# Normalising the softmax rows on GpSimd, and transposing them one group later

## The chip, the cores and the metric

The kernel runs on one core of a Trainium2 chip. The metric is the device time of one execution in microseconds (us). Most executions of a kernel agree within 0.3%. The engines are named as in the profile: PE is TensorE's matmuls and PEld its weight loads, DVE is VectorE, ACT is ScalarE, POOL is GpSimd, SP is the queue that only issues DMAs.

## The reference, cut to what matters

The input is x, 4 x 64 x 32 x 32. Two layers are computed: a Mamba-like convolution and scan block, then causal attention, and last a layer of 33 steps, each with a table of 19 sets of weights. A step picks its set by an argmax over the state, and masks say whether it does its attention, its feed-forward part, both or neither:

```python
def step(h, p):
    op = jnp.argmax(h[0, 0, :NOPS])
    q, k, v = h @ p['wq'][op], h @ p['wk'][op], h @ p['wv'][op]
    attn = jax.nn.softmax(jnp.einsum('bqd,bkd->bqk', q, k) * scale, axis=-1)
    y = jnp.einsum('bqk,bkd->bqd', attn, v) @ p['wo'][op]
    h = jnp.where(p['am'][op], y, h)
    z = jax.nn.relu(h @ p['w1'][op] + p['b1'][op]) @ p['w2'][op] + p['b2'][op]
    h = jnp.where(p['fm'][op], z, h)
    return (h, None)
```

With the inputs used here one step's attention runs, between two feed-forward parts. There are four sequences of 1024 tokens with 64 channels, all in float32. The attention has no causal mask.

## The kernel before, in words

Engines run their own programs and wait for each other through semaphores; the order of the work on each engine is written out by hand. Channels lie on partitions, two sequences at a time (rows r = 0 on partitions 0 to 63, r = 1 on 64 to 127), so that the four sequences are 2 x 2048 columns. One class, `Attention`, serves the causal attention of the layer before (`causal=True`, one pass, driven by code of its own) and that of the last layer (`ea`, `causal=False`), whose drivers are `pe_all`, `dve_all` and `act_all`. It goes over GRP = 16 groups g of 128 queries. For each group and each r:

- `pe_scores` (L242): four matmuls of 512 columns write the scores of 128 queries against 1024 keys into PSUM, `s[0]` and `s[1]` (`pb` in the trace). There is one pair of these tiles, so scores(g) wait until both exps of group g − 1 have read them.
- `dve_max_halves` (L343, L347, L349): row maxima, negated. For r = 0 two halves and their minimum, for r = 1 one pass over 1024.
- `act_exp` (L402): the exp of the scores into `p[g % 2][r]` in SBUF (`bb`, `dbu`), with the row sums in `sm`. Its read of the accumulator is an instruction of its own.
- `dve_inverse` (L367): `rc` = 1 / `sm`, for both r.
- `pe_turn` (L279): eight transposes of 128x128 of one `p` into the PSUM tile `pt` (`py`), of which there is one, 128 x 1024. Each half of four transposes is signalled on its own. Turn r = 1 may write a half once `dve_turned` has copied that half of r = 0 out, and the next r = 0 once the halves of r = 1 are out.
- `dve_turned` (L355) copies both halves of r = 0 into `pts` (`da`, `cc`), `act_turned` (L410) the first half of r = 1 and `dve_turned_rest` (L361) the second.
- `pe_values` (L292, L302): first two matmuls spread the inverse sums over partitions (L292: `rc` broadcast to 64 columns as weights, the identity as data) into columns 128 to 255 of the bank `ob` or `rb` (`px`), then 16 matmuls multiply the values `vv` with `pts` into columns 0 to 127.
- `act_inverse` (L416) copies the spread inverse to `rs`, and `output` (L107) multiplies the values' product by it. `finish` calls it three groups later.

In the steady state TensorE's order is scores(g), turn(g − 1, 1), values(g − 2), turn(g, 0). `hand_over` (L1764) copies four finished groups of output at a time. GpSimd has an empty `pool_attend`; what it does in this layer are sums of 512 columns in the feed-forward part (L1970). Behind the attention comes the feed-forward part, whose first TensorE work is L1044.

Of the kernel before, what the change touches and what calls it, by code (L numbers as in the profile page):

```python
# [45 lines left out]
class Attention:  # L46
# [4 lines left out]
    def __init__(self, nc, ctx, w, causal, bufs=None):  # L51
        tag = "l1_" if causal else "ex_"

        def sb(name, shape):
            return ctx.enter_context(nc.sbuf_tensor(tag + name, shape, FP32))

        def ps(name, shape):
            return ctx.enter_context(nc.psum_tensor(tag + name, shape, FP32))

        def sem(name):  # L60
            return ctx.enter_context(nc.semaphore(tag + name))

        self.nc, self.w, self.causal = nc, w, causal
        if bufs is None:
            bufs = {"qt": sb("qt", [128, T2C]), "kt": sb("kt", [128, T2C]), "vv": sb("vv", [128, self.GRP, 2, C]),
                    "p": [[sb(f"p_{a}{r}", [128, L]) for r in range(2)] for a in range(2)],
                    "pts": [[sb(f"pts_{a}{r}", [128, L]) for r in range(2)] for a in range(2)],
                    "rs": sb("rs", [128, 2, 128]), "nm": sb("nm", [128, 4]), "mh": sb("mh", [128, 2]), "sm": sb("sm", [128, 4]), "rc": sb("rc", [128, 4]),
                    "s": [ps(f"s_{r}", [128, L]) for r in range(2)], "pt": ps("pt", [128, L]),
                    "ob": ps("ob", [128, HALF]), "rb": ps("rb", [128, HALF])}  # L70
        self.qt, self.kt, self.vv, self.p, self.pts = (bufs[name] for name in ("qt", "kt", "vv", "p", "pts"))
        self.rs, self.nm, self.mh, self.sm, self.rc = (bufs[name] for name in ("rs", "nm", "mh", "sm", "rc"))
        self.s, self.pt, self.ob, self.rb = (bufs[name] for name in ("s", "pt", "ob", "rb"))
        self.q_full, self.q_out = sem("q_full"), sem("q_out")
        if causal:
            self.k_full, self.k_out = sem("k_full"), sem("k_out")
        else:
            self.fold_full, self.fold_act, self.fold_dve = sem("fold_full"), sem("fold_act"), sem("fold_dve")
        self.v_full, self.v_act, self.v_dve = sem("v_full"), sem("v_act"), sem("v_dve")
        self.s_full, self.nm_done, self.p_done = sem("s_full"), sem("nm_done"), sem("p_done")  # L80
        self.turned, self.pts_dve, self.pts_act = sem("turned"), sem("pts_dve"), sem("pts_act")
        self.rc_done, self.o_full, self.o_out = sem("rc_done"), sem("o_full"), sem("o_out")
        self.rb_out = sem("rb_out")


    def prime(self, eng, *counts):
# [6 lines left out]
            pe.sem_inc(sem, count)  # L93

    def prime_act(self, act):
        for sem, count in ((self.q_out, 2), (self.fold_act, 2), (self.v_act, 2), (self.p_done, 2 * self.GRP), (self.pts_act, self.GRP), (self.rb_out, self.GRP)):
            act.sem_inc(sem, count)

    def prime_dve(self, dve):
# [3 lines left out]

    def output(self, dve, k, g, to):

        dve.wait_ge(self.rb_out, self.GRP * k + g + 1)
        self.nc.vector.tensor_tensor(to, (self.ob, self.rb)[g % 2][:, 0:128], self.rs[:, g % 2, :], ALU.mult).then_inc(self.o_out, 1)  # L107

    def blocks(self, g):
        return g % 8 + 1 if self.causal else L // 128  # L110
# [144 lines left out]
    def pe_turn(self, pe, k, g, r):  # L255

        nc = self.nc
        pe.wait_ge(self.p_done, 2 * (self.GRP * k + g) + r + 1)
        if g == 0 and r == 0 and not self.causal:
            for c in (2, 3):  # L260
                self.query_ready(pe, k, c)
# [21 lines left out]
    def pe_values(self, pe, k, g, early=None):  # L283
        nc, p, bank = self.nc, g // 8, (self.ob, self.rb)[g % 2]
        if g == 0 and not self.causal:
            pe.wait_ge(self.v_dve, 2 * k + 2)
            pe.wait_ge(self.v_act, 2 * k + 2)
        pe.wait_ge(self.rc_done, self.GRP * k + g + 1)
        atleast(pe, self.o_out, self.GRP * k + g - 1)
        for r in range(2):  # L290
            i = 2 * (g % 2) + r
            nc.tensor.matmul(bank[C * r:C * r + C, 128:256], self.rc[:, i:i + 1].broadcast_to((128, C)),  # L292
                             self.w["cst"][:, IDN:IDN + 128], start=True, stop=True)
# [12 lines left out]
    def pe_all(self, pe, k, src, wa, turned_w, v_wait):  # L306
        for g in range(self.GRP):
# [9 lines left out]
                self.pe_project_v(pe, k, src, wa[2], (0, 1))  # L317
            else:
                self.pe_scores(pe, k, g)
                self.pe_turn(pe, k, g - 1, 1)  # L320
            if g >= 2:
                self.pe_values(pe, k, g - 2)
            self.pe_turn(pe, k, g, 0)
            if g == 0:
                self.pe_project_v(pe, k, src, wa[2], (2, 3))
        self.pe_turn(pe, k, self.GRP - 1, 1)
        self.pe_values(pe, k, self.GRP - 2)
        self.pe_values(pe, k, self.GRP - 1)


    def dve_max(self, dve, k, g, r):
# [30 lines left out]

    def dve_inverse(self, dve, k, g):
        dve.wait_ge(self.p_done, 2 * (self.GRP * k + g) + 2)
        atleast(dve, self.o_full, self.GRP * k + g - 1)
        i = 2 * (g % 2)
        self.nc.vector.reciprocal(self.rc[:, i:i + 2], self.sm[:, i:i + 2]).then_inc(self.rc_done, 1)  # L367

    def dve_all(self, dve, k, wa, turned_w, finish, hand_over):
        last = self.GRP - 1  # L370
        for g in range(self.GRP):
            if g == 0:
                self.dve_fold(dve, k, turned_w[1], turned_w[2], wa[2])
            if 3 <= g < last:
                finish(dve, k, g - 3)
            self.dve_max_halves(dve, k, g)
            if g == 0:
                self.dve_project(dve, k, 3)
                self.dve_project_v(dve, k, (0,))
            else:  # L380
                self.dve_turned_rest(dve, k, g - 1)
            self.dve_turned(dve, k, g)
            self.dve_inverse(dve, k, g)
            if g == 0:
                self.dve_project_v(dve, k, (2,))
            if g in (10, 12):
                hand_over(dve, k, g // 2 - 5)
            if g == last:
                hand_over(dve, k, 2)
                finish(dve, k, g - 3)  # L390
        self.dve_turned_rest(dve, k, last)
        for g in range(last - 2, last + 1):
            finish(dve, k, g)
# [24 lines left out]
    def act_all(self, act, k, wa, turned_w):  # L418
        for g in range(self.GRP):
            if g == 0:  # L420
                self.act_fold(act, k, turned_w[0], wa[0])
                self.act_project(act, k, 0)
                self.act_project(act, k, 2)
            else:
                self.act_turned(act, k, g - 1)
            for r in range(2):
                self.act_exp(act, k, g, r)
            if g == 0:
                self.act_project_v(act, k, (1, 3))
            if g >= 2:  # L430
                self.act_inverse(act, k, g - 2)
        self.act_turned(act, k, self.GRP - 1)
        self.act_inverse(act, k, self.GRP - 2)
        self.act_inverse(act, k, self.GRP - 1)


def build_all(nc, w, inp, scr, out):

    ctx = ExitStack()
    with ctx:  # L440
# [1529 lines left out]
            nc.gpsimd.tensor_tensor(fin[c], t2[:, col(c)], hn[:, col(c)], ALU.add).then_inc(fin_done if c < NCH - 1 else fin_last, 1)  # L1970

        def pool_attend(pool, k, kf, e, n):
            pass

        def pool_feed(pool, k, ka, e, n, b):
            for c in range(NCH - 1):
# [28 lines left out]

        @block.gpsimd
        def _(pool):
            nc.gpsimd.memset(w["eps"][:, :], EPS).then_inc(ones_set, 1)
            nc.gpsimd.memset(w["mone"][:, :], -1.0).then_inc(ones_set, 1)
            nc.gpsimd.memset(natl[:, NP_:NV + 1, :], 0.0).then_inc(nat_set, 1)  # L2010
# [243 lines left out]
```

## Time and profile before

| what | value |
|---|---|
| time, median of 3 runs | 708.53 us (707.62 to 711.39) |
| the profiled execution, its own time | 711.64 us |
| its span | 709.8 us |
| mean granted TensorE clock | 0.961 of full speed |
| PE busy | 618.5 us, 87% |
| DVE busy | 581.7 us, 82% |
| ACT busy | 415.2 us, 59% |
| POOL busy | 451.1 us, 64% |

The span is the stretch between the profiled execution's first and last instruction, the time has what lies around it as well. Busy shares are means over the whole span, most of which is the scan of the first layer; the last layer begins at about 555 us. The profile names tiles by the buffers that they share: `pb` are the scores, `bb` and `dbu` are `p`, `py` is `pt`, `da` and `cc` are `pts`, `px` holds the outputs, `gate_all` the small columns (maxima, sums, inverses, `rs`), `w_xs` the attention's output.

### The profile page before, as it was taken

Reading aid. Unit: us, or ns where it says so; the run is one execution under the profiler, and the core shown is the slowest. Engines: PE = TensorE matmul, PEld = TensorE weight load, DVE = VectorE, ACT = ScalarE, POOL = GpSimd, SP = SyncE. Lnnn points to the kernel's source line nnn. Section 1 sums busy time; section 2 is a strip of 40 time slices with the busy share of each in tenths; the row PEclk is TensorE's granted clock in tenths of the full one; section 3 lists DMA queues with packets and bytes.
Section 4 is the critical chain, followed back from the end, with each engine's and each line's share of the span. In section 5 each row is a group of like instructions: output and inputs, shape, how many; then the busy total and the mean of one; then the engine's idle time right before and its main releaser. Section 6 shows DMA issues by size and latency. Waiting matters only on the chain.

```text
span 709.8 us, 10911 instructions
## 1 busy us (share of the span) xinstructions
PE 618.5 (87%) x3732; PEld 267.0 (38%) x3732; DVE 581.7 (82%) x622; ACT 415.2 (59%) x643; POOL 451.1 (64%) x240
## 2 busy tenths in 40 slices
PE   8889879889877888988878887988979999999996
PEld 3323222222222212222222222345756446777771
DVE  5799999999999999999999999364365457788755
ACT  4878777668567566766774663353445525544441
POOL 7599999999999999999999999510000220000002
PEclk9989999999999999989999999999899999999999
DMA  3876679686666675666666763000000000000001
GB/s 104 220 267 211 230 227 291 226 259 226 232 232 253 211 250 211 236 217 210 234 233 222 234 241 115 1 1 0 3 5 8 1 20 1 1 2 1 2 2 65
DMA packets 32107, 101.20 MB, mean 143 GB/s; under 512 B 6821, under 2 KB 7342, under 8 KB 32046
## 3 DMA queue, kind: packets, MB, share of 16 engines
q1 hardware_dynamic: 30486, 99.42, 41.6%
q10 hardware_dynamic: 1240, 0.88, 0.4%
q8 instruction: 33, 0.54, 0.3%
q14 instruction: 28, 0.23, 0.1%
q0 software_dynamic: 320, 0.13, 0.1%
HBM read 94.64 MB, written 2.10 MB: 136 GB/s over the span
## 4 chain that ended last, share of the span: by engine, by line
PE 44%; DVE 23%; issue 19%; ACT 7%; POOL 5%; DMA 1%; DVEq 0%; ACTq 0%; POOLq 0%
DVE hh_all L1641 9%; DVE pb L1636 8%; PE py L279 7%; PE pb L242 6%; PE px L302 5%; PE py L816 5%; POOL hc L1956 4%; PE pb L1044 2%; PE py L1068 2%; PE px L845 2%; PE pb L804 2%; POOL dbu L1967 2%; PE px L292 1%; DVE dtu_all L1615 1%; PE px L763 1%
## 5 line engine op out<-in xcount | busy, mean ns | idle before, releaser
L1956 POOL TENSOR_TENSOR hc<-hh_all,cc 128x1024 f32<-128x1024 f32 x128 | 298.5, 2355 | 6.3 <-DVE hh_all L1641 4.6
L1641 DVE TENSOR_TENSOR_SCAN hh_all<-da,pb 128x1024 f32<-128x1024 f32 x80 | 182.9, 2286 | 3.4 <-ACT da L1324 0.4
L1970 POOL TENSOR_TENSOR yg<-w_xs 128x512 f32<-128x512 f32 x10 | 12.6, 1266 | 227.1 <-DVE w_xs L1783 132.7
L816 PE MATMUL py<-hc,w_cst 64*64 64x512 f32 x1024 | 148.2, 639 | 8.5 <-DVE yg L1652 8.5
L1967 POOL TENSOR_TENSOR dbu<-bb,dtu_all 128x1024 f32<-128x1024 f32 x48 | 113.2, 2358 | 5.0 <-DMA bb<-scr 5.0
L1641 DVE TENSOR_TENSOR_SCAN hh_all<-pb,dbu 128x1024 f32<-128x1024 f32 x48 | 108.9, 2269 | 2.0 <-DVE dtu_all L1615 1.7
L1636 DVE TENSOR_TENSOR pb<-pb,dtu_all 128x1024 f32<-128x1024 f32 x80 | 97.1, 1214 | 3.7 <-PE pb L804 1.2
L804 PE MATMUL pb<-bc,w_sel 128*128 128x512 bf16 x160 | 51.8, 408 | 53.1 <-DVE hh_all L1641 53.0
L1324 ACT ACTIVATE da<-dt_all,w_aneg 128x1024 f32<-128x1024 f32 x80 | 89.8, 1138 | 2.7 <-DVE dt_all L1622 1.8
L1324 ACT ACTIVATE pb<-dt_all,w_aneg 128x1024 f32<-128x1024 f32 x48 | 53.6, 1116 | 64.3 <-DVE hh_all L1641 63.8
L816 PEld LDWEIGHTS py<-hc,w_cst 64*64 64x64 f32 x1024 | 31.2, 136 | 80.9 <-issue 54.4
L804 PEld LDWEIGHTS pb<-bc,w_sel 128*128 128x128 bf16 x160 | 11.0, 99 | 113.4 <-DVE hh_all L1641 83.8
L335 DVE TENSOR_REDUCE gate_all<-pb 128x1 f32<-128x128 f32 (+7 forms) x32 | 22.8, 752 | 19.6 <-PE pb L252 19.5
L279 PE MATMUL py<-w_cst,dbu 128*128 128x128 f32 x208 | 30.3, 286 | 8.1 <-ACT dbu L402 4.8
L402 ACT ACTIVATE bb<-pb,gate_all 128x1024 f32<-128x1024 f32 (+4 forms) x32 | 28.6, 898 | 7.8 <-DVE gate_all L335 7.8
L402 ACT ACTIVATE dbu<-pb,gate_all 128x1024 f32<-128x1024 f32 (+3 forms) x32 | 30.3, 952 | 4.8 <-DVE gate_all L335 4.8
L242 PE MATMUL pb<-w_xs,u_all 64*128 64x512 f32 x128 | 31.8, 615 | 0.0
L410 ACT ACTIVATE da<-py 128x512 f32<-128x512 f32 (+2 forms) x20 | 9.8, 510 | 37.3 <-PE py L279 37.1
L410 ACT ACTIVATE cc<-py 128x512 f32<-128x512 f32 (+1 forms) x20 | 10.7, 553 | 34.6 <-PE py L279 34.6
L355 DVE COPY da<-py 128x512 f32<-128x512 f32 (+2 forms) x28 | 16.1, 610 | 17.6 <-PE py L279 17.6
L279 PE MATMUL py<-w_cst,bb 128*128 128x128 f32 x192 | 27.2, 279 | 3.8 <-ACT bb L402 3.8
L279 PEld LDWEIGHTS py<-w_cst,dbu 128*128 128x128 f32 x208 | 23.2, 144 | 19.1 <-issue 12.4
(326 smaller groups left out, 1020.0 us busy)
## 6 DMA issues: line engine op xcount, KB each, us to landing
cc<-scr SPq DMA_DIRECT2D x128, 512.0 KB, 4.3
bb<-scr SPq DMA_DIRECT2D x48, 512.0 KB, 5.0
w_xs<-w_xm SPq DMA_DIRECT2D x8, 256.0 KB, 6.5
w_xs<-hc SPq DMA_DIRECT2D x6, 256.0 KB, 3.8
scr<-bcf SPq DMA_DIRECT2D x8, 128.0 KB, 4.6
out<-yg SPq DMA_DIRECT2D x4, 256.0 KB, 2.6
w_xst<-in_x SPq DMA_DIRECT2D x1, 512.0 KB, 4.6
w_cst<-in_consts ACTq DMA_DIRECT2D x1, 404.0 KB, 5.0
```

Of the source, the lines that this page charges most:

```text
L242: part = nc.tensor.matmul(self.s[r][:, o + a:o + a + m], self.qt[rows, g * 128:(g + 1) * 128], self.kt[rows, p * L + a:p * L + a + m], sta ...
L279: last = nc.tensor.transpose(self.pt[:, o + j:o + j + 128], self.p[g % 2][r][:, j:j + 128], self.w["cst"][:, IDN:IDN + 128])
L302: last = nc.tensor.matmul(bank[C * r:C * r + C, 0:128], self.vv[:, p * 8 + j, r, :], self.pts[g % 2][r][:, j * 128:(j + 1) * 128], start=( ...
L335: self.nc.vector.tensor_reduce(self.nm[:, i:i + 1], self.s[r][:, self.start(g):self.start(g) + 128 * self.blocks(g)], AX.X, ALU.max, negat ...
L402: self.nc.scalar.activation(self.p[g % 2][r][:, 0:n], self.s[r][:, self.start(g):self.start(g) + n], ACT.Exp, bias=self.nm[:, i:i + 1], ac ...
L804: last = nc.tensor.matmul(pb[u % 2][:, half(h)], w["sel"][:, n, :], bc3[q % 2][:, half(h)], start=True, stop=True)
L816: last = nc.tensor.matmul(py[part(t), half(r)], ident[part(r), part(r)], hc[u % NHC][part(r), half(t)], start=(n == 0), stop=(n == NS - 1) ...
L1324: nc.scalar.activation(to[:, :], dt[q % 2][:, :], ACT.Exp, scale=w["aneg"][:, n:n + 1]).then_inc(da_done, 1)
L1636: nc.vector.tensor_tensor(pb[u % 2][:, :], pb[u % 2][:, :], dtu[q % 2][:, :], ALU.mult).then_inc(dbu_done, 1)
L1641: nc.vector.tensor_tensor_scan(hh[u % NHH][:, :], decay[:, :], drive[:, :], 0.0, ALU.mult, ALU.add).then_inc(scan_done, 1)
L1956: nc.gpsimd.tensor_tensor(hc[u % NHC][:, :], hh[u % NHH][:, :], cc[u % NCC][:, :], ALU.mult).then_inc(hc_done, 1)
L1967: nc.gpsimd.tensor_tensor(dbu[k % NDB][:, :], bb[k % 2][:, :], dtu[q % 2][:, :], ALU.mult).then_inc(pooled_done, 1)
```

## The change

In the non-causal attention only, the rows of `p` are multiplied by their inverse sums on GpSimd, in place, before they are transposed. So TensorE no longer spreads the inverse (L292), ScalarE no longer copies it (L416), and `output` is a plain copy. The transposes of a group wait for GpSimd (`p_norm`) instead of ScalarE, and all of them come one group later: TensorE's order becomes scores(g), turn(g − 1, 0), values(g − 2), turn(g − 1, 1). VectorE's copies of r = 0 move behind the maxima of the group after, and behind them the output and the reciprocal. The second pair of value projections moves from group 0 to group 1. After the last scores come values(14), both turns of group 15 and values(15).

```diff
     def output(self, dve, k, g, to):
-        dve.wait_ge(self.rb_out, self.GRP * k + g + 1)
-        self.nc.vector.tensor_tensor(to, (self.ob, self.rb)[g % 2][:, 0:128], self.rs[:, g % 2, :], ALU.mult).then_inc(self.o_out, 1)
+        bank = (self.ob, self.rb)[g % 2]
+        if self.causal:
+            dve.wait_ge(self.rb_out, g + 1)
+            self.nc.vector.tensor_tensor(to, bank[:, 0:128], self.rs[:, g % 2, :], ALU.mult).then_inc(self.o_out, 1)
+        else:
+            dve.wait_ge(self.o_full, self.GRP * k + g + 1)
+            self.nc.vector.tensor_copy(to, bank[:, 0:128]).then_inc(self.o_out, 1)
+
+    def pool_normed(self, pool, k, g, passed):
+        settle(pool, self.rc_done, self.GRP * k + g + 1, passed)
+        for r in range(2):
+            i = 2 * (g % 2) + r
+            self.nc.gpsimd.tensor_scalar(self.p[g % 2][r][:, :], self.p[g % 2][r][:, :], self.rc[:, i:i + 1], None, ALU.mult).then_inc(self.p_norm, 1)
...
     def pe_turn(self, pe, k, g, r):
-        pe.wait_ge(self.p_done, 2 * (self.GRP * k + g) + r + 1)
+        pe.wait_ge(self.p_done if self.causal else self.p_norm, 2 * (self.GRP * k + g) + r + 1)
...
     pe_values:
-        pe.wait_ge(self.rc_done, self.GRP * k + g + 1)
+        if self.causal:
+            pe.wait_ge(self.rc_done, g + 1)
         atleast(pe, self.o_out, self.GRP * k + g - 1)
-        for r in range(2):
+        for r in range(2 if self.causal else 0):
...
     pe_all:
             else:
                 self.pe_scores(pe, k, g)
+                self.pe_turn(pe, k, g - 1, 0)
+                if g == 1:
+                    self.pe_project_v(pe, k, src, wa[2], (2, 3))
+                else:
+                    self.pe_values(pe, k, g - 2)
                 self.pe_turn(pe, k, g - 1, 1)
-            if g >= 2:
-                self.pe_values(pe, k, g - 2)
-            self.pe_turn(pe, k, g, 0)
-            if g == 0:
-                self.pe_project_v(pe, k, src, wa[2], (2, 3))
-        self.pe_turn(pe, k, self.GRP - 1, 1)
-        self.pe_values(pe, k, self.GRP - 2)
-        self.pe_values(pe, k, self.GRP - 1)
+        last = self.GRP - 1
+        self.pe_values(pe, k, last - 1)
+        self.pe_turn(pe, k, last, 0)
+        self.pe_turn(pe, k, last, 1)
+        self.pe_values(pe, k, last)
...
     dve_inverse:
-        atleast(dve, self.o_full, self.GRP * k + g - 1)
+        if self.causal:
+            atleast(dve, self.o_full, g - 1)
+        else:
+            dve.wait_ge(self.p_norm, 2 * (self.GRP * k + g) - 2)
...
     dve_all:
-            if 3 <= g < last:
-                finish(dve, k, g - 3)
+            if g >= 2:
+                self.dve_turned_rest(dve, k, g - 2)
             self.dve_max_halves(dve, k, g)
             if g == 0:
                 self.dve_project(dve, k, 3)
                 self.dve_project_v(dve, k, (0,))
             else:
-                self.dve_turned_rest(dve, k, g - 1)
-            self.dve_turned(dve, k, g)
+                self.dve_turned(dve, k, g - 1)
+            if g == 1:
+                self.dve_project_v(dve, k, (2,))
+            if 3 <= g < last:
+                finish(dve, k, g - 3)
             self.dve_inverse(dve, k, g)
-            if g == 0:
-                self.dve_project_v(dve, k, (2,))
...
+        self.dve_turned_rest(dve, k, last - 1)
+        self.dve_turned(dve, k, last)
         self.dve_turned_rest(dve, k, last)
...
     act_all:
-            else:
-                self.act_turned(act, k, g - 1)
+            if g >= 2:
+                self.act_turned(act, k, g - 2)
             for r in range(2):
                 self.act_exp(act, k, g, r)
-            if g == 0:
-                self.act_project_v(act, k, (1, 3))
-            if g >= 2:
-                self.act_inverse(act, k, g - 2)
+            if g < 2:
+                self.act_project_v(act, k, (2 * g + 1,))
...
         def pool_attend(pool, k, kf, e, n):
-            pass
+            for g in range(GRP):
+                ea.pool_normed(pool, k, g, passed)
```

## Rows read from the trace of the kernel before

**Rows 1.** The page's part 1: busy us (share of the span) xinstructions.

```profile
PE 618.5 (87%) x3732; PEld 267.0 (38%) x3732; DVE 581.7 (82%) x622; ACT 415.2 (59%) x643; POOL 451.1 (64%) x240
```

**Rows 2.** Busy by window: length, PE, PEld, DVE, ACT, POOL, clock, DMA share, GB/s.

```profile
603.30:609.40 6.10, 6.10 (x63) 4.36 (x62) 4.81 (x10) 2.99 (x6) 0.00 (x0) 1.00 0.01 1
```

**Rows 3.** The chain that ended last, 598 to 688 us, by line.

```profile
by line: PE py L279 32.8%; PE px L302 30.9%; PE pb L242 29.1%; PE px L292 6.5%; DVE cc L355 0.8%; issue 0.1%
```

**Rows 4.** Timeline of one group: start us, us, engine and instruction, [idle before].

```profile
615.44 0.30 PEld L242 LDWEIGHTS pb<-w_xs,u_all 64*128 64x128 f32 x4 [0.16 <-issue]
...
616.61 0.69 DVE L343 TENSOR_REDUCE gate_all<-pb 128x1 f32<-128x512 f32 x1
617.36 0.86 PEld L279 LDWEIGHTS py<-w_cst,bb 128*128 128x128 f32 x8 [0.76 <-issue]
...
618.29 1.23 DVE L349 TENSOR_REDUCE gate_all<-pb 128x1 f32<-128x1024 f32 x1
618.38 0.20 PEld L292 LDWEIGHTS px<-w_cst,gate_all 128*64 128x64 f32 x4 [0.17 <-issue]
...
618.55 1.78 PEld L302 LDWEIGHTS px<-cc,w_xs 128*64 128x64 f32 x32
...
619.43 0.68 DVE L361 COPY da<-py 128x512 f32<-128x512 f32 x1
...
620.50 0.86 PEld L279 LDWEIGHTS py<-w_cst,dbu 128*128 128x128 f32 x8 [0.17 <-issue]
...
620.69 0.19 ACT L402 ACTIVATION_READ_ACCUMULATOR dbu<-pb,gate_all 128x1 f32 x1
...
621.52 0.30 PEld L242 LDWEIGHTS pb<-w_xs,u_all 64*128 64x128 f32 x4 [0.16 <-issue]
...
622.40 0.15 DVE L367 RECIPROCAL gate_all<-gate_all 128x2 f32<-128x2 f32 x1
```

**Rows 5.** Timeline, scores(2) behind the second exp of group 1.

```profile
596.95 0.21 ACT L402 ACTIVATION_READ_ACCUMULATOR dbu<-pb,gate_all 128x1 f32 x1
597.21 0.30 PEld L242 LDWEIGHTS pb<-w_xs,u_all 64*128 64x128 f32 x4 [0.23 <-ACT dbu L402]
```

**Rows 6.** Timeline, the stage's last group and the step behind it.

```profile
676.24 0.30 PEld L242 LDWEIGHTS pb<-w_xs,u_all 64*128 64x128 f32 x4 [0.16 <-issue]
...
682.00 1.29 DVE L355 COPY cc<-py 128x512 f32<-128x512 f32 x2 [1.09 <-PE py L279]
682.74 0.42 PEld L279 LDWEIGHTS py<-w_cst,dbu 128*128 128x128 f32 x4 [0.58 <-DVE cc L355]
...
683.27 0.40 DVE L1764 COPY w_xs<-w_xs 128x512 f32<-128x512 f32 x1
683.34 0.42 PEld L279 LDWEIGHTS py<-w_cst,dbu 128*128 128x128 f32 x4 [0.18 <-DVE cc L355]
...
683.99 0.23 PEld L292 LDWEIGHTS px<-w_cst,gate_all 128*64 128x64 f32 x4 [0.24 <-issue]
...
684.03 0.69 DVE L361 COPY cc<-py 128x512 f32<-128x512 f32 x1 [0.16 <-PE py L279]
...
688.10 0.30 PEld L1044 LDWEIGHTS pb<-w_xs,hc 64*128 64x128 f32 x4 [0.17 <-issue]
```

**Rows 7.** GpSimd: timeline from 15.74, then groups by line.

```profile
15.74 1.45 POOL L2045 TENSOR_SCALAR hc<-hh_all,w_vcol 128x1024 f32<-128x1024 f32 x1 [3.54 <-DVE hh_all L1687]
...
16.53 0.68 DVE L1662 BATCH_NORM_STATS2 stats<-w_xst 128x6 f32<-128x512 f32 x1
...
19.62 1.19 POOL L2045 TENSOR_SCALAR hc<-hh_all,w_vcol 128x1024 f32<-128x1024 f32 x1 [2.42 <-DVE w_scol L1657]
...
L1956 POOL TENSOR_TENSOR hc<-hh_all,cc 128x1024 f32<-128x1024 f32 x128 | 298.5, 2355 | 6.3 <-DVE hh_all L1641 4.6
...
L1994 POOL TENSOR_SCALAR gate_all<-gate_all 1x627 f32<-1x627 f32 x1 | 1.8, 1794 | 0.1
```

**Rows 8.** Timeline, group 0: the second exp's accumulator read.

```profile
589.14 0.21 ACT L402 ACTIVATION_READ_ACCUMULATOR bb<-pb,gate_all 128x1 f32 x1
```

More of the change, by code:

```diff
@@ L82, in __init__ @@
         self.rc_done, self.o_full, self.o_out = sem("rc_done"), sem("o_full"), sem("o_out")
-        self.rb_out = sem("rb_out")
+        if causal:
+            self.rb_out = sem("rb_out")
+        else:
+            self.p_norm = sem("p_norm")
     def prime(self, eng, *counts):
@@ L95, in prime_act @@
     def prime_act(self, act):
-        for sem, count in ((self.q_out, 2), (self.fold_act, 2), (self.v_act, 2), (self.p_done, 2 * self.GRP), (self.pts_act, self.GRP), (self.rb_out, self.GRP)):
+        for sem, count in ((self.q_out, 2), (self.fold_act, 2), (self.v_act, 2), (self.p_done, 2 * self.GRP), (self.pts_act, self.GRP)):
             act.sem_inc(sem, count)
@@ L364, in dve_inverse @@
         dve.wait_ge(self.p_done, 2 * (self.GRP * k + g) + 2)
-        atleast(dve, self.o_full, self.GRP * k + g - 1)
+        if self.causal:
+            atleast(dve, self.o_full, g - 1)
+        else:
+            dve.wait_ge(self.p_norm, 2 * (self.GRP * k + g) - 2)
         i = 2 * (g % 2)
@@ L423, in act_all @@
                 self.act_project(act, k, 2)
-            else:
-                self.act_turned(act, k, g - 1)
+            if g >= 2:
+                self.act_turned(act, k, g - 2)
             for r in range(2):
                 self.act_exp(act, k, g, r)
-            if g == 0:
-                self.act_project_v(act, k, (1, 3))
-            if g >= 2:
-                self.act_inverse(act, k, g - 2)
-        self.act_turned(act, k, self.GRP - 1)
-        self.act_inverse(act, k, self.GRP - 2)
-        self.act_inverse(act, k, self.GRP - 1)
+            if g < 2:
+                self.act_project_v(act, k, (2 * g + 1,))
+        for g in range(self.GRP - 2, self.GRP):
+            self.act_turned(act, k, g)
 def build_all(nc, w, inp, scr, out):
@@ L2007, in _ @@
         def _(pool):
+            ea.prime(pool, (ea.p_norm, 2 * GRP))
             nc.gpsimd.memset(w["eps"][:, :], EPS).then_inc(ones_set, 1)
```

## The prediction

> **What bounds the kernel now.** I read the page first: TensorE is busy for 87% of the span [rows 1]. That mean covers stages with different limits, and the change touches one stage alone, the non-causal attention between about 583 and 688 us. So next I took the busy times of one of its groups of 128 columns: in 6.10 us TensorE is busy for 6.10, VectorE for 4.81, ScalarE for 2.99, GpSimd for nothing, at a full granted clock [rows 2]. TensorE bounds this stage and GpSimd lies idle. The chain of waits through the stage agrees: all but 1% of it is TensorE's lines, and the spreading of the inverse (L292) has 6.5% of it [rows 3]. Then the timeline of one group, to have the order of the steps. With S the first weight load of `pe_scores`(g) at 615.44, the weight loads of the next pieces come at +1.92 (turn r = 1 of the group before), +2.94 (L292), +3.11 (values), +5.06 (turn r = 0) and +6.08 (the next scores) [rows 4]. The period is 6.08 us, and no step waits for another engine.
>
> A second circle is hidden under it: scores(g+1) need both exps of group g. From scores to the end of the second exp's accumulator read is 620.88 − 615.44 = 5.44 us [rows 4], and where TensorE had to wait for it, its weights went in 0.05 us after that read's end [rows 5]. So 5.49 us is a floor of the period, in both kernels. I use 0.05 us for every hand-over between engines whose wait ends with the end of an instruction.
>
> **What is removed.** TensorE loses the two L292 matmuls: the values' loads would start 618.55 − 618.38 = 0.17 us earlier, so TensorE's own sum falls from 6.08 to 5.91. ScalarE loses `act_inverse`, 0.27 us or so, worth nothing, as it is half idle [rows 2]. VectorE's multiply becomes a copy of the same size, also nothing.
>
> **What moving the transposes does.** This is where most of the 0.17 could go. The new order on TensorE is scores(g), turn(g−1, 0), values(g−2), turn(g−1, 1): +0, +1.92, +2.94, +4.89. Turn(g−1, 1) uses the PSUM tile that `dve_turned`(g−1) must first have copied out. VectorE now does that copy behind the three maxima of group g. The last maximum starts at 618.29, S + 2.85, and what follows it starts 1.14 later [rows 4]: the copies start at S + 3.99. The end of the stage before shows exactly this wait. Copies start at 682.00, TensorE is released for the first half at 682.74 and for the second at 683.34, 1.34 us behind the copies' start [rows 6]. So the second half of turn(g−1, 1) goes in at S + 5.33. Eight transposes there take 0.86 of loads and 0.16 to the next kind [rows 4], so four take 0.43 + 0.16 = 0.59, and scores(g+1) start at S + 5.92. In the end rows the same step took 683.99 − 683.34 = 0.65 [rows 6], which gives 5.98. New period: 5.92 to 5.98, where TensorE's own sum would allow 5.91. I take 5.95. The gain is 0.13 us per period. The copies are the new limit, just past TensorE.
>
> VectorE has to be back for the first maximum of g+1 in time: its last piece, the rest copy, can start 0.69 after the second half's loads (683.34 to 684.03) [rows 6], at S + 6.02, and takes 0.68 [rows 4], so ends at S + 6.70. That maximum starts 1.17 us behind its scores now (616.61) [rows 4], so at S + 7.12. No stall.
>
> **What is added: 32 multiplies on GpSimd.** No row shows this instruction here. The nearest is GpSimd's scale and shift of 128x1024 floats by two per-partition columns: 1.19 and 1.45 us [rows 7]. The longer of these ran from 15.74, while VectorE was reading the same memory (a statistics pass of 512 at 16.53, itself at 0.68). From above there are two bounds: the two-input product of the same size, 2.355 us, and a multiply by a constant of 627 elements on one partition, 1.794 us, whose rate of 2.86 ns would make 2.93 us of 1024 [rows 7]. I take 1.2 to 1.45, as shape, types and the column operand are those of the nearest row; 2.93 stays as the far end.
>
> Is it in time? The accumulator of exp(g, 1) is out at S + 5.44; the reciprocal starts at 5.49 and takes 0.15 [rows 4]; GpSimd starts at S + 5.69 and with a duration D is seen by TensorE at S + 5.74 + D. TensorE wants it at turn(g, 0), S + 5.95 + 1.92 = S + 7.87. So up to D = 2.13 there is no stall, and with 1.2 to 1.45 some 0.7 to 0.9 us are spare. The second multiply is wanted 3 us later still. Nothing else is queued behind these waits on GpSimd: its next work is the sums of the feed-forward step.
>
> On the price the Trainium skill cuts both ways. Its page "GPSIMD Engine Reference", section "Elementwise — side-by-side cycle accounting", gives about 2.6 cycles an element, an estimate of 2.2 us for 1024; the sum below would move by under 0.5 us. Its section "Engine selection" calls one-input work roughly line-rate, and with that the 1.19 us row agrees.
>
> **The start.** Before, scores(1) stand behind turn(0, 0) and the second pair of value projections; in the new order they come ahead of both, once exp(0, 1) is out: 589.14 + 0.21 + 0.05 = 589.40 [rows 8]. Multiplies of 1.2 us from about 589.6 are done by 590.8, ahead of turn(0, 0) at 589.40 + 1.92. Before, scores(2) start at 597.21 [rows 5]; now at 589.40 + 5.95 = 595.35. The start gains 1.9 us.
>
> **The end.** Before, from scores(15) at 676.24 to the feed-forward's first load at 688.10 are 11.86 us [rows 6]. Now the last group stands a whole turn later. From S: the rest copy of 14 starts at about 6.1, behind the reciprocal, a hand-over copy of 0.40 (started 0.3 before the next) [rows 6] and an output; it ends at 6.8. Values(14) 6.85, turn(15, 0) 8.80, copies 9.49, the second half of turn(15, 1) 9.49 + 1.34 = 10.83, rest copy 11.52 to 12.20, values(15) 12.25 and 1.95 more: 14.20. The end costs 14.20 − 11.86 = 2.34 us. This is the price of the shift by one group: nothing is left to cover it.
>
> **The sum.** Start −1.86, thirteen periods of −0.13 make −1.69, end +2.34: −1.2 us. Checked by clock: 589.40 + 14 x 5.95 + 14.20 = 686.90, against 688.10. With a period of 5.92 it is −1.6, with 5.98 −0.8. What follows (the feed-forward step, the store) is unchanged. The profiled execution would go from 711.64 to 710.4; it lies 3.1 above the median of the runs, 708.53, and I take the same difference from that: 707.3.
>
> **Rivals.**
> - *GpSimd is dear and becomes the wait.* Turn(g, 0) then starts at S + 5.74 + D, and 1.02 + 1.95 + 0.43 + 0.59 = 3.99 later come scores(g+2), so the mean period is (9.73 + D)/2. It binds from D = 2.13 on and eats all the gain at a mean period of 6.04, D = 2.34. At D = 2.36 the result is about +0.2; at 2.93 it is 14 x 6.33 − 84.5 = +4.1, and the last group's second multiply makes the end 1.2 longer: +5.3 us. It costs over 3.5 us from D = 2.73 on. For it: 2.86 ns an element in one row, in-place writing and the VectorE overlap, both unmeasured. Against: the 1.19 us row. Chance 0.12.
> - *The copy circle is longer than I have it.* Each 0.1 us on the way maximum, copy, transposes costs 14 x 0.1 = 1.4 us: a VectorE slowed by GpSimd at work, or later releases. With 6.1 to 6.2 for the period it gives +0.9 to +2.3. Against: the statistics pass beside GpSimd at its normal 0.68. Chance 0.13.
> - *TensorE gets back more.* The chain charges L292 6.5% of 90 us over 16 groups, 0.37 each [rows 3]. If the period fell by all of that to 5.71 and the copies gave way as well, the result would be 14 x 5.71 + 14.20 − 98.70 = −4.6 us. Against: the copies' 5.92. Chance 0.06.
>
> **How the numbers follow.** My forecast (−0.4 to −1.8, so 706.7 to 708.1) has 0.65; the rivals 0.13, 0.12, 0.06; 0.04 is left for the unforeseen. Without the −4.6 below and the dearest GpSimd above, and with the runs' own spread, the range is 705.2 to 710.6. About 0.5%, 3.5 us, is what this kernel's measurement can tell. Faster by more takes the third rival or luck of the runs, 0.09; slower by more the dear GpSimd or a copy circle far out, 0.11; within, 0.80.
>
> **What the profile would show.** Scores 5.92 to 5.98 apart, started each time after a wait of the second half of turn r = 1 for VectorE's copy; values straight behind turn r = 0; GpSimd's multiplies at 1.2 to 1.45 us, never what TensorE waits for; scores(1) near 589.4; from scores(15) to the feed-forward 14.2. The forecast fails if a multiply takes over 2.1 us, if scores are more than 6.04 apart, or if the end costs more than the 2.3 us counted.

## The result, and the profile after

The changed kernel takes 715.98 us (median of 5 runs, 715.28 to 717.53) against 708.53 of the kernel before (5 runs, 707.62 to 711.39). The ratio is 1.0087, with a 95% interval of 1.0063 to 1.0111: slower by 0.9%, where I had forecast 707.3 and no change that can be measured.

The profiled execution took 715.98 us. Its page, parts 1 and 5 (for a group: busy time, mean ns of one, idle time before):

```profile
span 714.1 us, 10799 instructions
...
PE 612.0 (86%) x3668; PEld 261.3 (37%) x3668; DVE 585.7 (82%) x622; ACT 413.8 (58%) x627; POOL 542.3 (76%) x272
...
L122 POOL TENSOR_SCALAR bb<-bb,gate_all 128x1024 f32<-128x1024 f32 x16 | 45.4, 2849 | 21.2 <-DVE gate_all L388 21.2
...
L122 POOL TENSOR_SCALAR dbu<-dbu,gate_all 128x1024 f32<-128x1024 f32 x16 | 45.4, 2847 | 2.2 <-DVE gate_all L388 2.2
```

Beside [rows 1] TensorE is down by 6.5 us of busy time and GpSimd up by 91. The 32 multiplies (L122) take 2.85 us each. I had put them at 1.2 to 1.45.

Single executions differ in the long stages ahead of this one: scores(0) start at 583.48 us in the trace of before and at 579.81 in this one, though the change leaves the work ahead of them as it was. So below I compare the length of the stage, from the first weight load of scores(0) to the feed-forward's first load. It was 688.10 − 583.48 = 104.62 us before. The start, in the timeline of the changed kernel (start us, us, engine):

```profile
579.81 0.30 PEld L257 LDWEIGHTS pb<-w_xs,u_all 64*128 64x128 f32 x4
...
585.73 0.30 PEld L257 LDWEIGHTS pb<-w_xs,u_all 64*128 64x128 f32 x4 [0.42 <-ACT bb L426]
...
586.17 5.68 POOL L122 TENSOR_SCALAR bb<-bb,gate_all 128x1024 f32<-128x1024 f32 x2 [12.27 <-DVE gate_all L388]
...
589.23 0.86 PEld L294 LDWEIGHTS py<-w_cst,bb 128*128 128x128 f32 x8 [2.34 <-issue]
```

Scores(1) come 5.92 us behind scores(0), exactly as forecast (589.40 − 583.48). But turn(0, 0), at 589.23, was to follow at 1.92, and comes at 3.50: the first of the two multiplies ends only at about 589.0 (586.17 + half of 5.68). Two groups of the steady state:

```profile
606.01 0.30 PEld L257 LDWEIGHTS pb<-w_xs,u_all 64*128 64x128 f32 x4 [0.17 <-issue]
...
611.33 0.19 ACT L426 ACTIVATION_READ_ACCUMULATOR bb<-pb,gate_all 128x1 f32 x1
...
611.64 0.17 DVE L388 RECIPROCAL gate_all<-gate_all 128x2 f32<-128x2 f32 x1
611.99 0.30 PEld L257 LDWEIGHTS pb<-w_xs,u_all 64*128 64x128 f32 x4 [0.17 <-issue]
...
612.01 5.66 POOL L122 TENSOR_SCALAR bb<-bb,gate_all 128x1024 f32<-128x1024 f32 x2 [1.27 <-DVE gate_all L388]
...
614.91 0.86 PEld L294 LDWEIGHTS py<-w_cst,bb 128*128 128x128 f32 x8 [1.76 <-POOL bb L122]
...
615.97 1.28 DVE L373 COPY da<-py 128x512 f32<-128x512 f32 x2
...
617.83 0.86 PEld L294 LDWEIGHTS py<-w_cst,bb 128*128 128x128 f32 x8 [0.17 <-issue]
...
618.85 0.30 PEld L257 LDWEIGHTS pb<-w_xs,u_all 64*128 64x128 f32 x4 [0.16 <-issue]
...
620.81 0.86 PEld L294 LDWEIGHTS py<-w_cst,dbu 128*128 128x128 f32 x8 [0.80 <-POOL dbu L122]
```

Read it from scores(4) at 606.01. The read of the second exp's sum ends at 611.52, the reciprocal runs from 611.64 to 611.81, GpSimd starts at 612.01, 6.00 us behind scores(4). The first multiply ends at about 614.86, and turn(4, 0) starts at 614.91. From there values(3), turn(4, 1) and scores(6) need 3.94 us. So two periods take 12.84 us, 6.42 each, against 6.08 before [rows 4].

The idle times in brackets are not all lost: before, the loads of this turn also stood 0.76 us behind those of the scores, with nothing to wait for, and began 1.92 us behind the first of them [rows 4]. Here turn(4, 0) begins 2.92 us behind scores(5) (611.99), so 1.00 us is lost to GpSimd. Turn(5, 0), in the other group of the pair, begins 1.96 us behind scores(6), so that wait of 0.80 us costs 0.04. And in the chain of waits of the stage (598 to 692 us, by line) GpSimd's lines have 21%, where TensorE's had all but 1% [rows 3]:

```profile
by line: POOL bb L122 18.3%; PE py L294 16.9%; PE px L318 15.8%; issue 14.7%; PE pb L257 14.6%; DVE cc L373 6.8%; DVE gate_all L361 4.4%; POOL dbu L122 3.1%; DVE w_xs L115 1.6%; DVE gate_all L388 1.3%; DVE gate_all L365 0.5%; DVE gate_all L
```

The end:

```profile
676.42 0.30 PEld L257 LDWEIGHTS pb<-w_xs,u_all 64*128 64x128 f32 x4 [0.17 <-issue]
...
682.35 5.71 POOL L122 TENSOR_SCALAR dbu<-dbu,gate_all 128x1024 f32<-128x1024 f32 x2 [0.24 <-DVE gate_all L388]
...
688.18 0.86 PEld L294 LDWEIGHTS py<-w_cst,dbu 128*128 128x128 f32 x8 [1.28 <-DVE cc L373]
...
692.37 0.30 PEld L1065 LDWEIGHTS pb<-w_xs,hc 64*128 64x128 f32 x4 [0.17 <-issue]
```

From scores(15) to the feed-forward's first load are 15.95 us, against 11.86 before [rows 6] and 14.20 forecast; turn(15, 1) starts at 688.18, when its multiply has just ended (682.35 + 5.71 = 688.06). The stage is 692.37 − 579.81 = 112.56 us, 7.9 longer than before.

### The profile page after: what moved, and what is told of

The parts are those of the page before. It is cut to its first block, busy times and chain, and to the rows that moved or that the text cites. A ratio compares the mean times of both kernels' runs of the same rounds, so it can differ in the third digit from the quotient of the medians.

```text
span 714.1 us, 10799 instructions
## 1 busy us (share of the span) xinstructions
PE 612.0 (86%) x3668; PEld 261.3 (37%) x3668; DVE 585.7 (82%) x622; ACT 413.8 (58%) x627; POOL 542.3 (76%) x272
## 4 chain that ended last, share of the span: by engine, by line
PE 37%; DVE 24%; issue 20%; POOL 9%; ACT 8%; DMA 1%; DVEq 1%; ACTq 0%; POOLq 0%
DVE hh_all L1662 9%; DVE pb L1657 7%; PE py L837 5%; PE py L294 5%; PE pb L257 5%; POOL hc L1977 4%; PE px L318 3%; POOL bb L122 3%; PE pb L1065 2%; PE py L1089 2%; PE px L866 2%; PE pb L825 2%; PE px L784 1%; POOL dbu L1988 1%; DVE dtu_all L1636 1%
## 5 line engine op out<-in xcount | busy, mean ns | idle before, releaser
L837 PE MATMUL py<-hc,w_cst 64*64 64x512 f32 x1024 | 146.6, 633 | 9.9 <-DVE yg L1673 9.9
L122 POOL TENSOR_SCALAR bb<-bb,gate_all 128x1024 f32<-128x1024 f32 x16 | 45.4, 2849 | 21.2 <-DVE gate_all L388 21.2
L122 POOL TENSOR_SCALAR dbu<-dbu,gate_all 128x1024 f32<-128x1024 f32 x16 | 45.4, 2847 | 2.2 <-DVE gate_all L388 2.2
L361 DVE TENSOR_REDUCE gate_all<-pb 128x1 f32<-128x512 f32 x32 | 22.1, 692 | 9.0 <-PE pb L257 9.0
```

Source lines behind the costliest of these rows:

```text
L122: self.nc.gpsimd.tensor_scalar(self.p[g % 2][r][:, :], self.p[g % 2][r][:, :], self.rc[:, i:i + 1], None, ALU.mult).then_inc(self.p_norm, 1)
L837: last = nc.tensor.matmul(py[part(t), half(r)], ident[part(r), part(r)], hc[u % NHC][part(r), half(t)], start=(n == 0), stop=(n == NS - 1) ...
```

## The experiments

D is the mean duration of one multiply, the period that of scores in the steady state (two values where they alternate), "end" the time from scores(15) to the feed-forward's first load. Ratios are against the kernel before, on the same chip as the run; where none is given there was one run, and those of two_input and one_input_free stand on two runs. half_rows, half_values and rows_800 leave a part of the work out, so they show times only and are no kernels to use.

| kernel | D, us | period, us | end, us | stage, us | ratio (95% interval) |
|---|---|---|---|---|---|
| before | none | 6.08 | 11.86 | 104.62 | |
| changed | 2.85 | 5.98 and 6.86 | 15.95 | 112.56 | 1.0087 (1.0063 to 1.0111) |
| fast_form | 1.21 | 5.90 | 14.61 | 103.13 | 0.9964 (0.9943 to 0.9985) |
| other_buffer | 2.85 | 5.97 and 6.86 | 15.94 | 112.53 | 1.0076 (1.0049 to 1.0103) |
| order_alone | none | 6.08 | 14.71 | 105.57 | 1.0005 (0.9986 to 1.0025) |
| half_rows | 1.57 | 5.90 | 14.61 | 103.15 | 0.9955 (0.9940 to 0.9970) |
| fast_form_end | 1.20 | 5.90 | 13.49 | 102.03 | 0.9958 (0.9931 to 0.9984) |
| two_input | 1.90 | 6.73 | 17.05 | 118.17 | 1.0162 (1.0095 to 1.0228) |
| mult_mult | 1.20 | 5.90 | 14.61 | 103.15 | |
| add_constant | 1.12 | 5.90 | 14.61 | 103.14 | |
| two_input_free | 1.90 | 5.93 | 14.64 | 104.08 | 0.9987 (0.9966 to 1.0008) |
| one_input_free | 2.85 | 6.07 and 6.73, later 6.25 and 6.58 | 15.97 | 112.25 | 1.0105 (1.0033 to 1.0176) |
| half_values | 1.20 | 5.90 | 14.23 | 102.80 | |
| rows_800 | 2.29 | 6.20 | 14.98 | 108.22 | 1.0060 (1.0046 to 1.0074) |

### What makes the multiply slow: its form or its place

**fast_form.** `zcol` is a column of zeros, set once at the start.

```diff
-tensor_scalar(p, p, self.rc[:, i:i + 1], None, ALU.mult)
+tensor_scalar(p, p, self.rc[:, i:i + 1], self.w["zcol"][:, :], ALU.mult, ALU.add)
```

> The changed kernel, but GpSimd's multiply by the inverse is written as multiply by the column and add a column of zeros (two operations, two per-partition columns, as in the scale and shift that took 1.19 and 1.45 us); still in place. Stage = from the first weight load of scores(0) to the feed-forward's first load: 104.6 us in the kernel before, 112.6 in the changed one. Theory A (the one-operation form is what is slow, at about 2.8 ns a column): the multiply takes 1.2 to 1.45 us, TensorE never waits for GpSimd, scores stand 5.92 to 5.98 apart, the stage is 103.4 us, the time 1.2 us under the kernel before. Theory B (writing in place, or VectorE at work beside it, is what makes it slow): the multiply stays near 2.85 us and the time near 716.

Theory A held. GpSimd's group in the view by lines (busy, mean ns):

```profile
L122 POOL TENSOR_SCALAR bb<-bb,gate_all,zcol 128x1024 f32<-128x1024 f32 x16 | 19.2, 1206 | 36.2 <-DVE gate_all L388 36.2
```

The one addition of zero takes the multiply from 2.85 to 1.21 us. With it the rest of the forecast is right: periods of 5.90 (5.92 to 5.98 forecast), a stage of 103.13 us (103.4), and a kernel faster than before by 0.36%.

**other_buffer.** The one-operation multiply, written into four free tiles, from which the transposes read.

```diff
-tensor_scalar(self.p[g % 2][r][:, :], self.p[g % 2][r][:, :], ...)
+tensor_scalar(self.pn[g % 2][r], self.p[g % 2][r][:, :], ...)
```

> The changed kernel with its one-operation multiply, but GpSimd writes the scaled rows into another buffer, from which the transposes read; nothing is written in place. Theory A (form): the multiply stays at 2.85 us and the time near 716. Theory B (in place): it falls to 1.2 to 1.45 us, and the stage from 112.6 to 103.4.

D stayed at 2.85 us and the stage at 112.53. Writing in place costs nothing. Nor is it VectorE's work beside the multiply: that was the same beside fast_form's 1.21 us.

**half_rows.** The multiply as in the change, over 512 columns; the others stay without their inverse.

```diff
-tensor_scalar(self.p[g % 2][r][:, :], self.p[g % 2][r][:, :], ...)
+tensor_scalar(self.p[g % 2][r][:, 0:HALF], self.p[g % 2][r][:, 0:HALF], ...)
```

> The changed kernel, but each multiply covers only the first 512 of 1024 columns (the other half of each row stays without its inverse). Theory A: the multiply takes about 512 x 2.78 ns = 1.45 us, under the 2.1 us from which it is waited for; stage about 103.4 us as in fast_form. If the price is a fixed one and not one per column, it stays well above 2 us and the stage above 106.

1.57 us for 512 columns and 2.85 for 1024: the slope is (2.85 − 1.57) / 512 = 2.50 ns a column, on 0.29 us fixed. The stage was 103.15, as with the fast form: what matters is how long the multiply takes, not how it is written.

**mult_mult** has ALU.mult with a column of ones in place of adding zero, **add_constant** adds the constant 0.0 in place of a column.

```diff
+mult_mult:    tensor_scalar(p, p, rc, ones_column, ALU.mult, ALU.mult)
+add_constant: tensor_scalar(p, p, rc, 0.0, ALU.mult, ALU.add)
```

> As fast_form, but multiply by the column and multiply by a column of ones. If any two operations are fast: 1.2 us and a stage of 103.1. If only multiply with add is: above 2.5 us, stage 110 or more.

> As fast_form, but the second operand is the constant 0.0 in the instruction and not a column: multiply by the column, add 0.0. If the pair multiply and add is what is fast: 1.2 us, stage 103.1. If both operands have to be columns: above 2.5 us, stage 110 or more.

1.20 and 1.12 us. Neither the pair multiply and add nor a second column is what it takes: with a column for the first operand, each form with two operations that I tried is fast, and the form with one is slow. It is no rule for every `tensor_scalar` with two operations: in the trace of before one with two constants (L1998, 627 elements on one partition) takes 2.35 us, more than the multiply by one constant over the same elements (1.79 [rows 7]).

### What the order costs by itself

**order_alone.** The new order, with the normalisation of the kernel before.

```diff
-pe.wait_ge(self.p_norm, ...)           # pe_turn
+pe.wait_ge(self.p_done, ...)
+# pe_values: the two L292 matmuls; act_all: act_inverse(g - 2); output: product with rs
-# pool_attend: pool_normed
```

> The new order of transposes, values and copies alone: TensorE spreads the inverse again, ScalarE copies it, the output is the product, GpSimd does nothing in the stage and the transposes wait for the exps. Theory A (GpSimd's price is the whole loss): TensorE's own sum sets the period, 6.08 us, the copies' circle of 5.92 is hidden under it, the start gains 1.9 and the end costs 2.3 to 2.7: stage 105.4 us, time +0.5 to +1.2 us against the kernel before. Theory C (the new order is what costs, GpSimd only adds): periods of 6.3 or more and a stage of 109 us or more.

The periods are TensorE's sum again, from one scores to the next:

```profile
615.45 0.30 PEld L250 LDWEIGHTS pb<-w_xs,u_all 64*128 64x128 f32 x4 [0.16 <-issue]
...
621.53 0.30 PEld L250 LDWEIGHTS pb<-w_xs,u_all 64*128 64x128 f32 x4 [0.16 <-issue]
```

The stage is 105.57 us (105.4 forecast): start −1.9, no period changed, end +2.85. The new order by itself costs 0.95 us of stage, which the ratio of 1.0005 (0.9986 to 1.0025) is too wide to show. Theory C fell.

### The circle through GpSimd, and one more wait

**rows_800.** As half_rows, over 800 of the 1024 columns.

```diff
+tensor_scalar(self.p[g % 2][r][:, 0:800], self.p[g % 2][r][:, 0:800], ...)
```

> The changed kernel, one-operation form, multiplies over 800 of 1024 columns (the rest of each row stays without its inverse). From 1.57 us at 512 and 2.85 at 1024 follows 2.29 us at 800. If the circle through GpSimd is 9.99 + D for two periods, their mean is 6.14 and the stage 5.92 + 14 x 6.14 + 14.9 = 106.8 us, half way between fast_form (103.1) and the changed kernel (112.6) or a little under; time about 2.2 us over the kernel before.

D was 2.29 us as worked out, but the period 6.20 and not 6.14, and the stage 108.22 and not 106.8. The loss grows with D, but the rest of the circle grew too:

```profile
L122 POOL TENSOR_SCALAR bb<-bb,gate_all 128x800 f32<-128x800 f32 x16 | 36.5, 2291 | 24.0 <-DVE gate_all L388 24.0
...
L365 DVE TENSOR_TENSOR gate_all<-gate_all 128x1 f32<-128x1 f32 x10 | 4.0, 403 | 0.3
```

VectorE's minimum of two columns (L365, in the second row) takes 0.40 us here in the mean. Before, it took 0.16:

```profile
L347 DVE TENSOR_TENSOR gate_all<-gate_all 128x1 f32<-128x1 f32 x11 | 1.7, 159 | 0.4
```

The exps wait for it. One group of rows_800:

```profile
617.82 0.30 PEld L257 LDWEIGHTS pb<-w_xs,u_all 64*128 64x128 f32 x4 [0.17 <-issue]
...
620.56 0.37 DVE L365 TENSOR_TENSOR gate_all<-gate_all 128x1 f32<-128x1 f32 x1
...
623.25 0.19 ACT L426 ACTIVATION_READ_ACCUMULATOR bb<-pb,gate_all 128x1 f32 x1
```

The second exp's sum is read out at 623.44, 5.62 us behind scores, against 5.51 in the changed kernel, whose minimum took 0.27 at that place (608.75). With these 0.11 us two periods are 9.99 + 2.29 + 0.11 = 12.39, or 6.20 each, as measured.

**two_input.**

```diff
-tensor_scalar(p, p, self.rc[:, i:i + 1], None, ALU.mult)
+tensor_tensor(p, p, self.rc[:, i:i + 1].broadcast_to((128, L)), ALU.mult)
```

> The changed kernel, with GpSimd's multiply as a product of two tensors, the second the inverse column read again for every element. The same kind took 2.36 us for 1024 columns in the scan. The circle by the changed kernel's rows: two periods take 9.99 + D, 12.84 at D = 2.85. If the circle is right, D = 2.36 gives periods of 6.18 in the mean, and a stage of 5.92 + 14 x 6.18 + 14.9 = 107.3 us, between fast_form (103.1) and the changed kernel (112.6); time about 2.7 over the kernel before. If the loss hangs on the form and not on D, it is 103 or 112.

This miss taught most. The product takes 1.90 us, less than 2.36 and far less than 2.85, and the kernel is the slowest of all: 118.17 us of stage. The timeline of one group:

```profile
627.98 0.30 PEld L257 LDWEIGHTS pb<-w_xs,u_all 64*128 64x128 f32 x4 [0.17 <-issue]
...
627.99 3.74 POOL L122 TENSOR_TENSOR bb<-bb,gate_all 128x1024 f32<-128x1024 f32 x2 [2.98 <-DVE gate_all L388]
...
630.73 1.02 DVE L365 TENSOR_TENSOR gate_all<-gate_all 128x1 f32<-128x1 f32 x1
...
631.67 1.21 DVE L367 TENSOR_REDUCE gate_all<-pb 128x1 f32<-128x1024 f32 x1
...
632.80 1.27 DVE L373 COPY da<-py 128x512 f32<-128x512 f32 x2
...
634.13 0.42 PEld L294 LDWEIGHTS py<-w_cst,bb 128*128 128x128 f32 x4 [0.18 <-DVE da L373]
...
634.71 0.30 PEld L257 LDWEIGHTS pb<-w_xs,u_all 64*128 64x128 f32 x4 [0.17 <-ACT dbu L426]
```

GpSimd's two products run from 627.99 to 631.73. VectorE's L365 needs 0.16 us when GpSimd is idle; here it takes 1.05 in the mean, and in this group it starts at 630.73, behind the maxima, and ends at 631.75, together with the second product. So it is in all 15 groups behind the first: it ends within 0.03 us of that product's end. The last maximum and the copies behind it are late by it: copies start at 632.80, 4.82 us behind scores at 627.98 (3.99 forecast), the second half of turn r = 1 at 634.13, the next scores at 634.71. The period of 6.73 is the copies' circle, made 0.83 us longer than fast_form's 5.90, and no longer GpSimd's.

**two_input_free.** The same kernel; the minimum takes its second input as a per-partition column.

```diff
-tensor_tensor(self.nm[:, i:i + 1], self.mh[:, 0:1], self.mh[:, 1:2], ALU.min)
+tensor_scalar(self.nm[:, i:i + 1], self.mh[:, 0:1], self.mh[:, 1:2], None, ALU.min)
```

> two_input was slower than the changed kernel (stage 118.2 us against 112.6) though its multiplies took 1.90 us instead of 2.85; there VectorE's minimum of the two half maxima (128x1, two inputs from SBUF) took 1.05 us instead of 0.16 and ended together with GpSimd's product. Here the same kernel with that minimum written as one input and one per-partition column. Theory D (VectorE's two-input instruction is held until GpSimd's two-input one is done): it takes 0.16 us again, two periods take 9.99 + 1.90 = 11.89, stage 5.92 + 14 x 5.95 + 14.6 = 103.8 us, time about 0.8 us under the kernel before. Rival (GpSimd's product slows VectorE whatever it does): the minimum or its neighbours stay long, and the stage above 110.

The stage falls by 14 us, to 104.08 (103.8 forecast), with products of 1.90 us as before. L365 takes 0.21:

```profile
L365 DVE TENSOR_SCALAR gate_all<-gate_all 128x1 f32<-128x1 f32 x10 | 2.1, 214 | 0.3
```

Theory D held: VectorE's instruction with two inputs from SBUF was held until GpSimd's two-input one was done. This agrees with the Trainium skill, "GPSIMD Engine Reference", section "Specifications", which names contention with VectorE instructions that have two SBUF inputs.

**one_input_free.** The changed kernel with the same rewritten minimum.

> The changed kernel with the same rewritten minimum; the multiply stays in its slow one-operation form. In the changed kernel the minimum took 0.16 in one group and 0.27 to 0.43 in the next. Theory D: with one-input multiplies the hold is small, so little changes: stage 111.6 to 112.5 us, multiplies still 2.85. Rival (the hold is a main part of the 8 us): stage 108 or less.

112.25 against 112.56: with the multiply of the change, which has one input, the hold is worth 0.3 us. It is not where the 8 us went.

### Which circle limits the good versions

**half_values.** fast_form with `n = 4` for 8 in `pe_values`: half of the values' product is left out.

```diff
-        n = self.blocks(g)
+        n = self.blocks(g) if self.causal else 4
```

> fast_form with the values' product over only 4 of 8 blocks of keys (the other half of the sum is left out), so TensorE's own sum falls by some 0.9 us a group, to 5.0. If the copies' circle (maxima, copy, second half of turn r = 1, next scores) is a limit of its own at 5.90 to 5.92, the period stays there. If TensorE's sum alone sets it, the period falls to the floor of the exps, about 5.5 us, and the stage by 5 us.

```profile
623.35 0.30 PEld L257 LDWEIGHTS pb<-w_xs,u_all 64*128 64x128 f32 x4 [0.17 <-issue]
...
626.29 0.85 PEld L318 LDWEIGHTS px<-cc,w_xs 128*64 128x64 f32 x16 [0.16 <-issue]
...
627.33 1.28 DVE L373 COPY da<-py 128x512 f32<-128x512 f32 x2
...
628.07 0.42 PEld L294 LDWEIGHTS py<-w_cst,bb 128*128 128x128 f32 x4 [0.92 <-DVE da L373]
...
628.66 0.42 PEld L294 LDWEIGHTS py<-w_cst,bb 128*128 128x128 f32 x4 [0.18 <-DVE da L373]
...
629.25 0.30 PEld L257 LDWEIGHTS pb<-w_xs,u_all 64*128 64x128 f32 x4 [0.17 <-issue]
```

The values' loads (L318) are down to 0.85 us, and TensorE then waits 0.92 for the first copy. The copies start at 627.33, 3.98 behind scores at 623.35, the second half of the turn goes in at 628.66, and the next scores at 629.25: the period is 5.90 with half of that work gone. The copies' circle is a limit of its own. In fast_form it and TensorE's sum coincide:

```profile
622.54 0.30 PEld L257 LDWEIGHTS pb<-w_xs,u_all 64*128 64x128 f32 x4 [0.17 <-issue]
...
624.46 0.86 PEld L294 LDWEIGHTS py<-w_cst,bb 128*128 128x128 f32 x8 [0.76 <-POOL bb L122]
...
627.38 0.89 PEld L294 LDWEIGHTS py<-w_cst,bb 128*128 128x128 f32 x8 [0.17 <-DVE da L373]
...
628.44 0.30 PEld L257 LDWEIGHTS pb<-w_xs,u_all 64*128 64x128 f32 x4 [0.17 <-issue]
```

Turn r = 1 starts at 627.38, 0.17 us behind the loads before it, which is the step that stood there before as well [rows 4], and with no second wait between its halves. The 0.76 us ahead of turn r = 0 are no wait for GpSimd either: it starts 1.92 us behind scores, as before [rows 4].

**fast_form_end.** fast_form, with another end.

```diff
-        self.pe_values(pe, k, last - 1)
         self.pe_turn(pe, k, last, 0)
         self.pe_turn(pe, k, last, 1)
+        self.pe_values(pe, k, last - 1)
         self.pe_values(pe, k, last)
 ...
+        finish(dve, k, last - 2)
         self.dve_turned(dve, k, last)
         self.dve_turned_rest(dve, k, last)
-        for g in range(last - 2, last + 1):
+        for g in range(last - 1, last + 1):
```

> fast_form with another end: both turns of group 15 ahead of values(14), and the output of group 13 ahead of VectorE's copies of group 15. In fast_form the end (from scores(15) to the feed-forward's first load) took 14.61 us: TensorE waited 1.22 us for the rest copy of group 14, and values(15) 1.38 for the rest copy of 15 and the output of 13. Worked out from its rows: turn(15, 0) at scores(15) + 7.2, turn(15, 1) from 8.6, values(14) 9.8, values(15) 11.8, end 13.7. Theory (the end's cost is the uncovered shift by one group): stage 103.1 - 0.9 = 102.2 us, time 0.9 us under fast_form and some 2.4 under the kernel before. Rival (the end is bound by what I do not see, or the moved turns wait for the multiplies): no change or slower.

```profile
669.07 0.30 PEld L257 LDWEIGHTS pb<-w_xs,u_all 64*128 64x128 f32 x4 [0.17 <-issue]
...
676.29 0.86 PEld L294 LDWEIGHTS py<-w_cst,dbu 128*128 128x128 f32 x8 [1.49 <-POOL dbu L122]
...
678.92 1.73 PEld L318 LDWEIGHTS px<-da,w_xs 128*64 128x64 f32 x32 [0.17 <-issue]
...
682.56 0.30 PEld L1068 LDWEIGHTS pb<-w_xs,hc 64*128 64x128 f32 x4 [0.17 <-issue]
```

Both turns of group 15 are done before values(14) start at 678.92, and values(15) follow without a wait. The end takes 13.49 us, 1.1 less than in fast_form, and the stage, 102.03, is the shortest of all. By the ratio (0.9958, 0.9931 to 0.9984) it is 0.4% faster than the kernel before; that it beats fast_form (0.9964) is seen in the stage only, as the intervals overlap.

## Why the prediction was wrong, point by point

**The step that failed** is the price of the added instruction: "I take 1.2 to 1.45, as shape, types and the column operand are those of the nearest row". I went by the row of the same size, and that row had two operations, where the added multiply has one. It took 2.85 us, past the 2.13 from which I had TensorE wait, and turn r = 0 came 1.00 us late in every second group. That the number of operations is the difference is shown by fast_form, mult_mult and add_constant (1.12 to 1.21 us) against other_buffer (2.85). The trace of before held the right price, in smaller multiplies by one column on GpSimd, which I did not use:

```profile
L2053 POOL TENSOR_SCALAR w_wts<-w_cst,w_scol 64x64 f32<-64x64 f32 x8 | 3.4, 437 | 0.4
...
L2056 POOL TENSOR_SCALAR w_wts<-w_cst,w_vcol 128x128 f32<-128x128 f32 x1 | 0.6, 602 | 0.1
```

From 64 to 128 columns (and as many partitions) the one-operation form takes 0.165 us more, 2.58 ns a column. Carried on to 1024 columns that is 0.602 + 896 x 0.00258 = 2.91 us. The third row that I did cite, 2.86 ns a column on one partition, was also of one operation, and I set it aside as the far end. The estimate of 2.2 us from the Trainium skill ("GPSIMD Engine Reference", "Elementwise — side-by-side cycle accounting") was nearer than my row, but by luck: the page gives that figure for a product of two tensors, which takes 2.36 us here [rows 7], and it is still below the 2.85 measured. Its "roughly line-rate" for one-input work, in the section "Engine selection", fits the forms with two operations here (1.12 to 1.21 us) and not the one with one.

**The first rival was what happened**, and was too cheap. At D = 2.85 its sum gives 14 x 6.29 for the periods and about 15.2 for the end, +4.6 us in all; measured by the stage it was +7.9, by the medians +7.5. From scores(1) to scores(15) the changed kernel takes 90.69 us, where 14 x 6.29 = 88.1. The pair of periods was 12.84 and not 9.73 + 2.85 = 12.58, since GpSimd started 6.00 us behind scores and not 5.69: the second exp's sum was out 0.07 later, the reciprocal started 0.12 behind it, not 0.05, took 0.17, not 0.15, and GpSimd started 0.20 behind the reciprocal, not 0.05. These sum to 0.31, less 0.05 by which the way from the turn on is shorter (3.94 for 3.99). That makes 1.8 of the 2.6 us; the rest is the first of them (7.27 us, where others of its kind took 6.86) and two of 6.14 and 6.19 us where the others of their kind took 5.98; why these are longer no run shows. The end has the last 0.7 us: 0.3 by the same hand-overs, and 0.4 by a wait that I had left out (below). The threshold from which GpSimd is waited for moves with it, from 2.13 us to about 2 x 5.90 − 9.99 = 1.81.

**Right, in mechanism and size:** the start (scores(1) at +5.92); that the copies behind the maxima become a limit next to TensorE's own sum (5.90 measured in half_values, 5.92 forecast); the period with a fast multiply (5.90 against 5.92 to 5.98). **Right in kind, too small:** the end, 14.61 us in fast_form for 14.20. The 0.4 us are values(15) waiting for the output of group 13, which VectorE does behind the last copies; I had left that order out. With the fast multiply these make the stage 1.5 us shorter than before, where the sum said 1.2.

**The second rival**, a longer copy circle, did not come by the change's own multiply (0.3 us, one_input_free), but two_input showed that GpSimd can do exactly that. **The third**, that TensorE gets back all the 0.37 us of L292, fell: order_alone against fast_form shows 6.08 − 5.90 = 0.18 us a group, about the 0.17 of the weight loads. Since fast_form's turn r = 1 has no wait, this is TensorE's own gain, and half_values shows that in this order the copies would hold the period at 5.90 even if TensorE got back more.

## What to carry to other kernels

Price an added instruction by rows of the same form, its number of operations included, and scale those by their slope in size; a row of the right size and another form can be wrong by more than a factor of two. When work goes to an idle engine, what counts is its latency in the circle (here free up to about 1.8 us, then half of each further microsecond in every period), so the hand-overs to and from it have to be counted as well. And look for the other engine's instructions with two inputs from SBUF: a product on GpSimd held one of 128x1 for a microsecond.

## What the runs showed of the hardware

- On GpSimd a `tensor_scalar` over 128x1024 floats with one operation took 2.85 us, with two operations 1.12 to 1.21, and with an added zero it is the same product. Each had one per-partition column as its first operand. Over 512, 800 and 1024 columns the one-operation form took 1.57, 2.29 and 2.85 us. The reason is not shown by any run.
- A product of two tensors on GpSimd took 1.90 us where the second input was one column read again, and 2.36 for two full tensors [rows 7].
- VectorE's two-input instruction of 128x1 took 1.05 us in the mean while GpSimd did products with one column read again, and ended with the second product. Beside one-operation multiplies of 2.29 us it took 0.40 in the mean and ended long before the multiply (620.93 against 622.28), and 0.16 where no multiply ran; VectorE's reductions and copies out of PSUM kept their times beside GpSimd (0.69, 1.22, 0.68).
- GpSimd started 0.20 us behind the end of VectorE's reciprocal, TensorE 0.05 us behind the end of GpSimd's multiply.
